# Two causal attentions of a four-layer kernel: the diagonal tiles of the maximum pass go out through ScalarE and GpSimd, and the weighting stands between the two score pairs

## The chip, the core and the metric

One core of a Trainium2 chip runs the whole kernel as one program. Its engines are TensorE (PE in the profile; PEld is its weight load), VectorE (DVE), ScalarE (ACT), GpSimd (POOL) and SyncE (SP, which only starts transfers). The metric is the device time of one execution in microseconds. Attention B_ and attention G_ are the same function, called twice; its tiles carry these letters in the profile.

## The reference

The program computes a grouped-query causal attention, a mixture of experts, an attention in which masks go by pages of 64 positions, and two layers of local attention with a gated unit, with layer norms between. The change touches only the first and the third. What they compute, for 2 sequences of 2048 positions and 16 heads of 16 columns:

```python
att = jnp.einsum('bsgmd,btgd->bgmst', q, k) / scale
att = jnp.where(causal, -jnp.inf, att)            # third layer: pages[None, :] <= pages[:, None] is kept
att = jax.nn.softmax(att, axis=-1)
ctx = jnp.einsum('bgmst,btgd->bsgmd', att, v).reshape(b, s, DIM)
```

## The kernel before, in words

`attention` works in 8 iterations, one for each sequence and group of 4 heads. Each iteration does two things for its four heads. First, scores with queries on partitions (tiles `pm`), of which only the maximum of each query over its keys is wanted; it is later subtracted through two extra rows of the query operand. Second, scores with keys on partitions (`psc`), their exponential (`p`, by ScalarE), and the weighting of the values into `po` (`weigh`). The queries and keys are stored as high and low parts stacked to 48 rows (50 with the maxima), heads alternating between partitions 0 and 64.

The second part is cut into 40 steps: four query chunks of 512, and for chunk qc the 4(qc+1) key blocks of 128 up to the diagonal. In the last four key blocks of a chunk the step is 512, 384, 256 and 128 columns wide. The first part is cut into tiles ("pieces") of one head by up to 512 keys, or two heads where the width is at most 256. A list `ring` holds the 144 pieces of an iteration in order of query block, and between them, for each chunk, a "fold" (VectorE brings the partial maxima together, GpSimd splits them into high and low part) and, 12 pieces after the chunk's last one, a "turn" (TensorE transposes them, ScalarE copies them out, SyncE sends them into the rows of the query operand). The pieces run 22 entries ahead: `cut[t]` gives the entries of step t, 3 or 4 of them, and the first 83 stand in an opening before the first step. Pieces and turns take three PSUM banks in rotation (`RING = 3`, `slots`); `free` makes TensorE wait until the former user of the bank has been read. One bank holds `po`; `psc` takes four.

TensorE's order in step t is: first score pair (heads 0 and 1), one ring entry, second score pair (heads 2 and 3), one ring entry, the weighting of step t-1, the other entries (lines 454 to 465). The score pair waits for the exponential of the same pair in the step before; the weighting waits for both exponentials of step t-1, in diagonal steps also for GpSimd's clearing of `p` (line 304 or 308), and in a chunk's first step for the copy of `po`.

VectorE takes the pieces in the same order. A piece that ends at the diagonal gets a `tensor_tensor_reduce` with a mask tile `far` for each head (line 510, followed in the profile by an accumulator read), any other one a plain maximum (line 515). The copy of `po` to `o` (line 528) stands on VectorE after the entries of a chunk's first step. ScalarE does the exponentials (line 491) and the copies of the turned maxima (line 479). In a step with a turn, SyncE first sends the two transfers of its maxima (line 355) and then, in a chunk's first step, stores the output of the chunk before (line 360); it takes its work strictly in order. In the fifth step GpSimd starts the 13 loads of the next iteration.

Of the kernel before, what the change touches and what calls it, by code (L numbers as in the profile page):

```python
# [6 lines left out]
F32 = mybir.dt.float32  # L7
# [8 lines left out]
P = 128  # L16
# [162 lines left out]
def attention(nc, sem, tag, nk, page, qh, ql, kh, kl, vs, mask_qk, ident_bf, ident, ot):  # L179
# [5 lines left out]
    AHEAD = 22  # L185

# [4 lines left out]
    pieces = []  # L191
    for qb in range(NQ):
        full, rest = divmod((qb + 1) * P, CH)
        for kc in range(full + (rest > CH // 2)):
            pieces += [(qb, kc, min(CH, (qb + 1) * P - kc * CH), [h]) for h in range(GRP)]
        if 0 < rest <= CH // 2:
            pieces += [(qb, full, rest, [u, u + 2]) for u in range(2)]
    NP = len(pieces)
    steps = [(qc, kb) for qc in range(NC4) for kb in range(SUB * (qc + 1))]
    NS = len(steps)  # L200
    closes = [max(j for j, pc in enumerate(pieces) if pc[0] // SUB == c) for c in range(NC4)]
    ring = []
    for j in range(NP):
        ring.append(("piece", j, 0))
        for behind, kind in ((1, "fold"), (12, "turn")):
            for c in range(NC4):
                if (closes[c] + behind) % NP == j:
                    ring.append((kind, c, (closes[c] + behind) // NP))
    NE = len(ring)
    slots, taken = [], 0  # L210
    for kind, _, _ in ring:
        slots.append(taken % RING)
        taken += kind != "fold"
    cut = [NE * (t + AHEAD) // NS for t in range(NS + 1)]

    def exists(k, e):

        return not isinstance(k, int) or 0 <= k - ring[e][2] < NIT

    def spread(i, t):  # L220

        return [(i + e // NE, e % NE) for e in range(cut[t], cut[t + 1]) if exists(i + e // NE, e % NE)]

    opening = [(0, e) for e in range(cut[0]) if exists(0, e)]

    with ExitStack() as ctx:
# [6 lines left out]
        mpart = sb("mpart", [P, 2, PAR, NQ, NC4], F32)  # L233
        mfold = sb("mfold", [P, 2, PAR, SUB], F32)
        m = sb("m", [P, P], F32R)
        mrow = sb("mrow", [2 * GRP * SUB, P], F32)
        one = sb("one", [2, CH], F32)
        mqk = sb("mqk", [P, P], BF16)
        far = sb("far", [P, CH], F32)
# [6 lines left out]
        m_mask, far_set, apart = sem(tag + "m_mask", 0), sem(tag + "far_set"), sem(tag + "apart")  # L246
        q_in = [sem(f"{tag}q_in{i}", 0) for i in range(2)]
        s_max, max_done = sem(tag + "s_max"), sem(tag + "max_done")
        folded, m_hi, m_all = sem(tag + "folded"), sem(tag + "m_hi"), sem(tag + "m_all")
# [29 lines left out]
        def _(pool):  # L279

            pool.dma_start(mqk[:], mask_qk).then_inc(m_mask, 16)
# [37 lines left out]
            def split(k, e, clears):  # L319
                kind, c, late = ring[e]  # L320
                if kind != "fold":
# [3 lines left out]
                wait_apart(pool, folded, (k - late) * NC4 + c + 1, fence)  # L325
                wait_apart(pool, mt_done, (k - late) * NC4 + c, fence)
                parts = m[:, 0:2 * GRP * SUB].rearrange("p (b r n) -> p r b n", b=2, r=2)
                whole = mfold[:].rearrange("p b a j -> p b (a j)")
                pool.tensor_copy(parts[:, 0], whole).then_inc(m_hi, 1)
                wait_apart(pool, m_hi, (k - late) * NC4 + c + 1, fence)  # L330
                pool.tensor_tensor(parts[:, 1], whole, parts[:, 0].bitcast(F32), ALU.subtract).then_inc(m_all, 1)
                wait_apart(pool, m_all, (k - late) * NC4 + c + 1, fence)

            for k, e in opening:
                split(k, e, None)

            def body(i, s, half):
                for t, (qc, kb) in enumerate(steps):
# [5 lines left out]
                    for k, e in spread(i, t):  # L344
                        split(k, e, i * NQ + masked(t + 1))
# [3 lines left out]
        def _(sp):  # L349
            def m_row(k, e, s):  # L350
                _, c, late = ring[e]
                sp.wait_ge(mr_done, (k - late) * NC4 + c + 2)
                s = (s + late) % 2
# [8 lines left out]
            for k, e in opening:  # L362
                if ring[e][0] == "turn":
                    m_row(k, e, 0)

            def body(i, s, half):
                for t, (qc, kb) in enumerate(steps):
                    for e in range(cut[t], cut[t + 1]):
                        if ring[e % NE][0] == "turn" and exists(i + e // NE, e % NE):
                            m_row(i + e // NE, e % NE, (s + e // NE) % 2)  # L370
# [11 lines left out]
        def _(pe):  # L382
            def free(k, e):

                for back in range(1, 2 * NE):
                    g = e - back
                    kk, n = k + g // NE, g % NE
                    if ring[n][0] != "fold" and slots_at(g) == slots[e] and exists(kk, n):
                        break
                    if isinstance(kk, int) and kk < 0:  # L390
                        return
                kind, j, late = ring[n]
                if kind == "piece":
                    pe.wait_ge(max_done, kk * NP + j + 2)
                else:
                    pe.wait_ge(mr_done, (kk - late) * NC4 + j + 2)

            def slots_at(g):

                return slots[g % NE]  # L400

            def event(k, e, s):
                kind, j, late = ring[e]
                if kind == "fold":
                    return
# [30 lines left out]
            def body(i, s, half):  # L436
                for t, (qc, kb) in enumerate(steps):
# [22 lines left out]
                    elif not static(i, 0):  # L460
                        weigh(i - 1, 1 - s, NS - 1)
# [1897 lines left out]
```

## Time and profile before

| | us |
|---|---|
| median of 3 runs | 5498.16 (5486.85 to 5507.22) |
| profiled execution | 5505.85 |
| its span, first to last instruction | 5504.3 |
| TensorE busy in the span | 4333.2 (79%) |
| VectorE busy | 3117.9 (57%) |
| ScalarE busy | 2342.5 (43%) |
| GpSimd busy | 1217.9 (22%) |

Busy time is the union of an engine's instructions; matmuls are pipelined, so TensorE's share overstates how much its array works. The granted clock of TensorE is given as a share of full speed. In a row, `A<-B,C` says which tile is written from which, and a bracket gives the idle time of the engine before the row and what ended it. Several instructions of a kind that follow each other are merged into one row with their number at its end.

### The profile page before, as it was taken

The numbers are of one execution on the slowest core, as the hardware profiler recorded it, in microseconds if no ns is written. First come the engines' busy times: TensorE is split into PE (matmuls) and PEld (weight loads), VectorE is DVE, ScalarE is ACT, GpSimd is POOL, SyncE is SP. The second block draws the span as 40 slices with busy tenths as digits, with TensorE's granted clock in tenths as the row PEclk, the third lists the DMA queues.
The fourth block names the chain that finished last, engine by engine and source line by source line (L and its number), as shares of the span: only waits on it lengthen the run. The fifth ranks groups of instructions, "written<-read, shape, count | busy, mean of one in ns | idle before, by whom it ended". The sixth has DMA issues, their size and how long they took to land. (4 is left out here: it accounts for less than half of the span.)

```text
span 5504.3 us, 82496 instructions
## 1 busy us (share of the span) xinstructions
PE 4333.2 (79%) x24804; PEld 2724.9 (50%) x24804; DVE 3117.9 (57%) x6686; ACT 2342.5 (43%) x4143; POOL 1217.9 (22%) x1610
## 2 busy tenths in 40 slices
PE   4899999952989995649989899657796976689687
PEld 2433433341888884324333334345565755566466
DVE  1787777641444442648777777267454437656444
ACT  1365555621444442214555555323454433355333
POOL 1011111015000002110111110123585003378300
PEclk9788878875999997777878776789898988899888
DMA  7211311023112112352223330233453113345211
GB/s 219 33 29 32 48 31 28 11 101 115 57 49 76 47 48 67 118 129 32 40 40 49 49 57 11 90 108 116 150 157 110 31 48 107 120 156 158 69 34 35
DMA packets 327165, 413.82 MB, mean 75 GB/s; under 512 B 40804, under 2 KB 236257, under 8 KB 323260
## 3 DMA queue, kind: packets, MB, share of 16 engines
q1 hardware_dynamic: 278620, 257.43, 14.9%
q0 software_dynamic: 43616, 148.19, 12.7%
q10 hardware_dynamic: 4608, 4.20, 0.2%
q8 instruction: 167, 2.74, 0.2%
q14 instruction: 154, 1.26, 0.1%
HBM read 252.64 MB, written 156.19 MB: 74 GB/s over the span
## 5 line engine op out<-in xcount | busy, mean ns | idle before, releaser
L491 ACT ACTIVATE G_p<-G_psc 128x1024 f32<-128x1024 f32 (+3 forms) x640 | 541.9, 894 | 426.0 <-PE G_psc L454 423.6
L491 ACT ACTIVATE B_p<-B_psc 128x1024 f32<-128x1024 f32 (+3 forms) x640 | 541.7, 894 | 370.7 <-PE B_psc L454 367.9
L515 DVE TENSOR_REDUCE G_mpart<-G_pm 128x1 f32<-128x512 f32 x768 | 485.2, 684 | 150.0 <-PE G_pm L416 148.2
L416 PE MATMUL G_pm<-G_ks,G_qs 48*128 48x512 f32 (+3 forms) x1280 | 491.2, 521 | 89.3 <-DMA G_ks<-G_one 58.7
L515 DVE TENSOR_REDUCE B_mpart<-B_pm 128x1 f32<-128x512 f32 x768 | 483.8, 684 | 98.6 <-PE B_pm L416 96.5
L416 PE MATMUL B_pm<-B_ks,B_qs 48*128 48x512 f32 (+3 forms) x1280 | 480.1, 506 | 74.5 <-DMA B_ks<-B_one 42.9
L1705 POOL TENSOR_SCALAR J_pr<-J_pr,J_rc 128x256 f32<-128x256 f32 x512 | 462.7, 915 | 41.2 <-DVE J_rc L1843 38.8
L416 PEld LDWEIGHTS G_pm<-G_ks,G_qs 48*128 48x128 f32 x1280 | 229.9, 227 | 478.4 <-DVE G_mpart L515 222.9
L416 PEld LDWEIGHTS B_pm<-B_ks,B_qs 48*128 48x128 f32 x1280 | 222.8, 218 | 450.4 <-DVE B_mpart L515 223.6
L431 PE MATMUL G_po<-G_p,G_v 128*32 128x512 f32 (+3 forms) x2560 | 371.2, 657 | 20.5 <-DVE G_o L528 18.9
L431 PE MATMUL B_po<-B_p,B_v 128*32 128x512 f32 (+3 forms) x2560 | 353.3, 628 | 21.9 <-DVE B_o L528 19.3
L454 PE MATMUL G_psc<-G_qs,G_ks 50*128 50x512 f32 (+3 forms) x1280 | 334.5, 452 | 41.9 <-DMA G_qs<-G_mrow 31.9
L454 PE MATMUL B_psc<-B_qs,B_ks 50*128 50x512 f32 (+3 forms) x1280 | 324.9, 440 | 13.3 <-issue 7.7
L510 DVE CUSTOM_DVE_ANT_0 G_pm<-G_pm,G_far 128x384 f32<-128x384 f32 (+3 forms) x512 | 238.8, 517 | 125.6 <-PE G_pm L416 124.4
L1060 ACT ACTIVATE E_hs<-E_pH,E_bf 128x512 f32<-128x512 f32 (+1 forms) x192 | 115.7, 602 | 434.6 <-PE E_pG L1014 434.6
L510 DVE CUSTOM_DVE_ANT_0 B_pm<-B_pm,B_far 128x384 f32<-128x384 f32 (+3 forms) x512 | 238.9, 518 | 105.7 <-PE B_pm L416 104.2
L1027 PE MATMUL E_pO<-E_wp,E_a 128*128 128x256 f32 (+1 forms) x1920 | 252.0, 296 | 57.8 <-DVE E_a L1089 52.3
L1574 POOL TENSOR_TENSOR I_t<-I_qn,I_R 128x512 f32<-128x512 f32 x128 | 166.7, 1323 | 512.8 <-DVE I_qn L1628 512.8
L1027 PEld LDWEIGHTS E_pO<-E_wp,E_a 128*128 128x128 f32 (+1 forms) x1920 | 246.7, 198 | 63.1 <-DVE E_a L1089 57.2
L1014 PE MATMUL E_pH<-E_xT,E_wfg 128*128 128x512 f32 (+1 forms) x1152 | 262.4, 364 | 19.7 <-DVE E_wfg L1099 15.6
L1014 PE MATMUL E_pG<-E_xT,E_wfg 128*128 128x512 f32 (+1 forms) x1152 | 255.7, 358 | 0.0
L1804 ACT ACTIVATE J_pr<-J_pS,J_nm 128x256 f32<-128x256 f32 x512 | 234.8, 477 | 38.9 <-DVE J_nm L1839 38.8
(307 smaller groups left out, 7962.1 us busy)
## 6 DMA issues: line engine op xcount, KB each, us to landing
J_v<-lve SPq DMA_DIRECT2D x64, 520.0 KB, 3.8
J_k<-lkT SPq DMA_DIRECT2D x64, 512.0 KB
lve<-I_v SPq DMA_DIRECT2D x64, 260.0 KB, 2.1
lqT<-I_tT SPq DMA_DIRECT2D x64, 256.0 KB, 2.4
lkT<-I_tT SPq DMA_DIRECT2D x64, 256.0 KB, 2.6
J_q<-lqT SPq DMA_DIRECT2D x64, 256.0 KB
ein<-Z_z SPq DMA_DIRECT2D x8, 1228.0 KB
E_xin<-ein POOLq DMA_DIRECT2D x8, 1152.0 KB, 6.3
```

Of the source, the lines that this page charges most:

```text
L416: last = pe.matmul(t[:, n * w:(n + 1) * w], qs[s][rows, qb // SUB, h // 2, qb % SUB * P:(qb % SUB + 1) * P], ks[s][rows, h // 2 % NA, kc * ...
L431: last = pe.matmul(po[VW * h:VW * (h + 1), off:CH], v[s][:, kb, h % nk], p[:, t % 2, h, off:CH], start=kb == 0, stop=kb == SUB * (qc + 1) - 1,
L454: score = pe.matmul(psc[:, h, off:CH], ks[s][rows, h // 2 % NA, kb * P:(kb + 1) * P], qs[s][rows, qc, h // 2, off:CH], start=True, stop=True)
L491: act.activation(p[:, t % 2, 2 * pr:2 * pr + 2, off:CH], psc[:, 2 * pr:2 * pr + 2, off:CH], ACT.Exp, scale=SC).then_inc(e_done[pr], 1)
L510: last = dve.tensor_tensor_reduce(pm[slots[e]][:, x * w:(x + 1) * w], pm[slots[e]][:, x * w:(x + 1) * w], far[:, CH - w:CH], 1.0, -3e38, A ...
L515: dve.tensor_reduce(mpart[:, heads[0] % 2, heads[0] // 2, qb, kc:kc + 1], pm[slots[e]][:, 0:w], AX, ALU.max).then_inc(max_done, 1)
L1014: last = pe.matmul(bank[ht % 2][:, 0:w], wfg_p[pw][:, i, kc, ht * P:(ht + 1) * P], xT[px][:, kc, 0:w], start=kc + j == 0, stop=kc == KC - ...
L1027: last = pe.matmul(pO[j // 2][0:r, j % 2 * D:(j % 2 + 1) * D], a[pa][:, ht, j * P:j * P + r], wp_p[pw][:, ht], start=ht + i == 0, stop=ht ...
L1060: act.activation(hs[:, ht % 2, 0:w], pH[ht % 2][:, 0:w], ACT.Identity, bias=bf[:, s, ht:ht + 1]).then_inc(hs_done, 1)
L1574: last = pool.tensor_tensor(t2[:, u, :, :, a:a + H], qn[:, u, :, :, z:z + H], R[:, :, ds(w_, 1), a:a + H].to_broadcast([P, 2, LH, H]), ALU ...
L1705: last = pool.tensor_scalar(pr[:, u, pos(h)], pr[:, u, pos(h)], rc[:, u, pos(h):pos(h) + 1], None, ALU.mult)
L1804: last = act.activation(pr[:, u, pos(h)], pS[:, pos(h)], ACT.Exp, bias=nm[:, u, pos(h):pos(h) + 1], scale=8.0, accum_out=su[:, u, pos(h):p ...
```

## The change

- The ring no longer has masked pieces. The pieces end before the diagonal block; the diagonal blocks of two query blocks and two heads form one entry "diag": four matmuls of 128 columns in one bank. An iteration has 128 pieces, 16 diagonal entries and 4 turns, 148 entries in all; folds are no entries any more.
- A diagonal entry is copied by ScalarE into one of four tiles `dm` in SBUF (`d_out`), masked there by GpSimd (`d_cut`; `affine_select` in B_, fills in G_), and VectorE takes its maximum, 512 columns at once, six entries later (`d_max`). ScalarE's copy frees the bank.
- The partial maxima get a fifth column per query block for the diagonal. Mask tile, mask transfer and `tensor_tensor_reduce` go; `wait_apart` goes from VectorE.
- Within the entries of a step the pieces come first, then diagonal entries and turns.
- TensorE's order in a step is: first score pair, one entry, the weighting of step t-1, second score pair, the other entries.
- ScalarE copies `po` out after the exponentials of a chunk's first step, ahead of its copies of diagonal entries and turns.
- The turn of the third chunk falls into the fifth step instead of the sixth, that of the first into the 25th instead of the 26th, that of the second into the 33rd instead of the 34th.

The core of the diff:

```diff
+    DSLOTS = 4
+    REDUCE_BEHIND, TURN_BEHIND = 6, 12
...
+        for kc in range(qb // SUB):
+            off += [("piece", (qb, kc, CH, [h])) for h in range(GRP)]
+        rest = qb % SUB * P
+        if rest > CH // 2:
+            off += [("piece", (qb, qb // SUB, rest, [h])) for h in range(GRP)]
+        elif rest:
+            off += [("piece", (qb, qb // SUB, rest, [u, u + 2])) for u in range(2)]
+        if qb % 2 == 0:
+            off = [("diag", (qb, 0))] + off[:2] + [("diag", (qb, 1))] + off[2:]
...
+        held = [order[e % NE] for e in range(cut[t], cut[t + 1])]
+        held = [x for x in held if x[0] == "piece"] + [x for x in held if x[0] != "piece"]
...
+            def cut_diagonal(k, e, clears):
+                if ring[e][0] != "diag" or not exists(k, 0):
                     return
+                d = number[e]
+                if clears is not None:
+                    wait_apart(pool, cleared, clears, fence)
+                wait_apart(pool, d_out, k * ND + d + 1, fence)
+                tile = dm[:, d % DSLOTS]
+                if page == 1:
+                    pool.affine_select(out=tile, in_=tile, pattern=[[0, 2 * PAR], [-1, P]], compare_op=ALU.is_ge,
+                                       fill=-3e38, base=0, channel_multiplier=1).then_inc(d_cut, 1)
...
+                if kind == "diag":
+                    qb, u = what
+                    parts = [(h, q, q * P, P) for h in (u, u + 2) for q in (qb, qb + 1)]
...
                         score.then_inc(s_done, 1)
-                        some(pr, pr + 1)
-                    if t:
-                        weigh(i, s, t - 1)
-                    elif not static(i, 0):
-                        weigh(i - 1, 1 - s, NS - 1)
-                    some(2, len(events))
+                        if pr == 0:
+                            some(0, 1)
+                            if t:
+                                weigh(i, s, t - 1)
+                            elif not static(i, 0):
+                                weigh(i - 1, 1 - s, NS - 1)
+                    some(1, NE)
...
+                if kind == "diag":
+                    d = number[e]
+                    act.wait_ge(s_max, k * NI + issued[e] + 2)
+                    if not static(k, 0) or d >= DSLOTS:
+                        act.wait_ge(d_max, k * ND + d + 2 - DSLOTS)
+                    act.activation(dm[:, d % DSLOTS], pm[slots[e]][:].rearrange("p (n k) -> p n k", k=P), ACT.Copy
+                                   ).then_inc(d_out, 1)
...
+            def copy_out(i, qc):
+                act.wait_ge(pv_done, i * NS + sum(SUB * (c + 1) for c in range(qc + 1)) + 1)
...
+                act.activation(o[:, qc % 2], po[:], ACT.Copy).then_inc(o_done, 1)
```

## Rows read from the trace of the kernel before

**Rows 1.** The page: busy time, share of the span, instructions of each engine.

```profile
PE 4333.2 (79%) x24804; PEld 2724.9 (50%) x24804; DVE 3117.9 (57%) x6686; ACT 2342.5 (43%) x4143; POOL 1217.9 (22%) x1610
```

**Rows 2.** Windows: us, busy us (instructions) per engine, granted clock, DMA share, GB/s.

```profile
149.50:197.20 47.70, 46.14 (x96) 24.10 (x97) 46.02 (x135) 0.53 (x2) 0.82 (x4) 0.50 0.40 46
...
197.20:1110.00 912.80, 846.15 (x5060) 354.45 (x5056) 692.01 (x1722) 546.70 (x670) 139.93 (x266) 0.84 0.17 28
...
2522.70:3493.00 970.30, 877.82 (x5060) 366.49 (x5056) 693.04 (x1722) 546.95 (x670) 97.70 (x266) 0.79 0.22 36
...
610.54:651.16 40.62, 38.48 (x259) 15.88 (x258) 36.18 (x90) 28.67 (x35) 3.19 (x7) 1.00 0.02 8
...
2968.70:3009.31 40.61, 38.45 (x259) 15.89 (x258) 36.17 (x90) 28.78 (x34) 1.65 (x6) 1.00 0.03 9
...
572.00:578.30 6.30, 5.58 (x41) 2.50 (x41) 6.30 (x14) 3.93 (x5) 0.63 (x1) 1.00 0.00 0
...
578.40:588.50 10.10, 10.10 (x44) 4.24 (x38) 5.20 (x12) 4.05 (x5) 0.00 (x0) 0.50 0.08 28
...
653.60:680.60 27.00, 26.06 (x115) 10.99 (x114) 17.25 (x40) 11.53 (x16) 10.31 (x19) 0.50 0.65 86
```

**Rows 3.** Timeline of B_, a high-clock step: start, us, engine, work [idle before].

```profile
705.31 0.50 PE L416 MATMUL B_pm<-B_ks,B_qs 48*128 48x512 f32 x2
...
705.64 0.40 PE L454 MATMUL B_psc<-B_qs,B_ks 50*128 50x512 f32 x2
...
705.84 1.29 DVE L515 TENSOR_REDUCE B_mpart<-B_pm 128x1 f32<-128x512 f32 x2 [0.21 <-PE B_pm L416]
...
706.08 1.94 ACT L491 ACTIVATE B_p<-B_psc 128x1024 f32<-128x1024 f32 x2 [0.75 <-PE B_psc L454]
...
706.59 0.50 PE L416 MATMUL B_pm<-B_ks,B_qs 48*128 48x512 f32 x1
...
707.02 1.06 PE L431 MATMUL B_po<-B_p,B_v 128*32 128x512 f32 x8
...
708.01 0.50 PE L416 MATMUL B_pm<-B_ks,B_qs 48*128 48x512 f32 x2
```

**Rows 4.** Timeline of B_, a low-clock step.

```profile
674.89 0.79 PE L416 MATMUL B_pm<-B_ks,B_qs 48*128 48x512 f32 x2
...
675.49 0.63 PE L454 MATMUL B_psc<-B_qs,B_ks 50*128 50x512 f32 x2
...
675.72 2.48 DVE L515 TENSOR_REDUCE B_mpart<-B_pm 128x1 f32<-128x512 f32 x4 [1.83 <-PE B_pm L416]
...
676.47 0.79 PE L416 MATMUL B_pm<-B_ks,B_qs 48*128 48x512 f32 x1
...
677.19 1.93 PE L431 MATMUL B_po<-B_p,B_v 128*32 128x512 f32 x8
...
679.06 0.79 PE L416 MATMUL B_pm<-B_ks,B_qs 48*128 48x512 f32 x2
```

**Rows 5.** Timeline of B_ where a query chunk begins.

```profile
576.95 0.69 DVE L528 COPY B_o<-B_po 128x512 f32<-128x512 f32 x1
...
577.78 1.42 PE L431 MATMUL B_po<-B_p,B_v 128*32 128x512 f32 x8 [0.72 <-DVE B_o L528]
```

**Rows 6.** Timeline of G_, SyncE's queue, then TensorE.

```profile
2903.62 1.31 SPq L355 DMA_DIRECT2D G_qs<-G_mrow  x2
...
2929.46 1.21 PE L454 MATMUL G_psc<-G_qs,G_ks 50*128 50x512 f32 x3 [5.72 <-DMA G_qs<-G_mrow]
```

**Rows 7.** Groups by line and form: busy us, mean ns | idle before, releaser.

```profile
L510 DVE CUSTOM_DVE_ANT_0 B_pm<-B_pm,B_far 128x512 f32<-128x512 f32 x128 | 86.0, 715 | 23.4 <-PE B_pm L416 22.8
...
L510 DVE DVE_READ_ACCUMULATOR2_ANT B_mpart<- 128x1 f32 x512 | 72.7, 142 | 0.0
...
L1810 ACT ACTIVATE J_pT<-J_pP 128x512 f32<-128x512 f32 x128 | 76.4, 597 | 276.3 <-PE J_pP L1763 276.3
...
L304 POOL TENSOR_SCALAR_AFFINE_SELECT B_p<-B_p 128x512 f32<-128x512 f32 x128 | 81.2, 634 | 467.8 <-ACT B_p L491 464.9 <-POOL B_m L331 2.9
```

More of the change, by code:

```diff
@@ L220, in spread @@
-    def spread(i, t):
-        return [(i + e // NE, e % NE) for e in range(cut[t], cut[t + 1]) if exists(i + e // NE, e % NE)]
-    opening = [(0, e) for e in range(cut[0]) if exists(0, e)]
+    order, close = [], {}
+    for qb in range(NQ):
+        off = []
+        for kc in range(qb // SUB):
[7 more added lines that the diff above has]
+            off = [("diag", (qb, 0))] + off[:2] + [("diag", (qb, 1))] + off[2:]
+        order += off
+        close[qb // SUB] = len(order) - 1
@@ new lines, in attention @@
+    NE = len(order) + NC4
+    late_of = {}
+    for c in reversed(range(NC4)):
+        at = close[c] + TURN_BEHIND
+        late_of[c] = int(at >= len(order))
+        order.insert(at % len(order), ("turn", c))
+    cut = [NE * (t + AHEAD) // NS for t in range(NS + 1)]
+    ring = [None] * NE
+    for t in range(NS):
+        held = [order[e % NE] for e in range(cut[t], cut[t + 1])]
+        held = [x for x in held if x[0] == "piece"] + [x for x in held if x[0] != "piece"]
+        for x, e in zip(held, range(cut[t], cut[t + 1])):
+            ring[e % NE] = x
@@ new lines, in attention @@
+    late = [late_of[x[1]] if x[0] == "turn" else 0 for x in ring]
+    number, count = [], {"piece": 0, "diag": 0, "turn": 0}
+    for kind, what in ring:
+        number.append(what if kind == "turn" else count[kind])
+        count[kind] += 1
+    NP, ND = count["piece"], count["diag"]
+    issued = [sum(x[0] != "turn" for x in ring[:e]) for e in range(NE)]
+    NI = NP + ND
+    slots = [e % RING for e in range(NE)]
+    if NE % RING == 1:
+        slots[-1] = 1
+    after = [[] for _ in range(NE)]
@@ new lines, in attention @@
+    last_of = {c: (0, 0, 0) for c in range(NC4)}
+    for e, (kind, what) in enumerate(ring):
+        if kind == "diag":
+            after[(e + REDUCE_BEHIND) % NE].append(("reduce", e, (e + REDUCE_BEHIND) // NE))
+        if kind != "turn":
+            c = what[0] // SUB
+            ready_at, pieces_done, diags_done = last_of[c]
+            if kind == "piece":
+                last_of[c] = (max(ready_at, e), number[e] + 1, diags_done)
+            else:
+                last_of[c] = (max(ready_at, e + REDUCE_BEHIND), pieces_done, number[e] + 1)
@@ L226, in attention, with exists, window @@
+    for c in range(NC4):
+        e = last_of[c][0] + 1
+        after[e % NE].append(("fold", c, e // NE))
+    def exists(k, back):
+        return not isinstance(k, int) or 0 <= k - back < NIT
+    def window(i, t):
+        return [(i + e // NE, e % NE) for e in range(cut[t], cut[t + 1])]
+    opening = [(0, e) for e in range(cut[0])]
     with ExitStack() as ctx:
@@ L362, in _ @@
             for k, e in opening:
-                if ring[e][0] == "turn":
+                if ring[e][0] == "turn" and exists(k, late[e]):
                     m_row(k, e, 0)
@@ L367, in body @@
                 for t, (qc, kb) in enumerate(steps):
-                    for e in range(cut[t], cut[t + 1]):
-                        if ring[e % NE][0] == "turn" and exists(i + e // NE, e % NE):
-                            m_row(i + e // NE, e % NE, (s + e // NE) % 2)
+                    for x in range(cut[t], cut[t + 1]):
+                        k, e = i + x // NE, x % NE
+                        if ring[e][0] == "turn" and exists(k, late[e]):
+                            m_row(k, e, (s + x // NE) % 2)
                     if kb == 0:
@@ L524, in copy_out @@
-            def copy_out(i, qc):
-                dve.wait_ge(pv_done, i * NS + sum(SUB * (c + 1) for c in range(qc + 1)) + 1)
-                if not (isinstance(i, int) and i == 0 and qc < 2):
-                    dve.wait_ge(o_out[qc % 2], i * (NC4 // 2 * 16) + qc // 2 * 16 + 1)
-                dve.tensor_copy(o[:, qc % 2], po[:]).then_inc(o_done, 1)
-            dve.memset(mpart[:], -3e38)
-            dve.memset(far[:], 0.0).then_inc(far_set, 1)
-            dve.wait_ge(far_set, 2)
-            dve.wait_ge(m_mask, 16)
```

204 lines of the change are left out of this document (93 added, 111 removed).

## The prediction

> **What bounds the kernel now.** I read the page first (VectorE busy 3117.9 of 5504.3 us, TensorE 4333.2) [rows 1]: neither share names a bound. Both attentions together last, after their openings, 912.8 + 970.3 us, and only they and their openings (47.7 us in B_) are touched by the change [rows 2]. Each holds 8 iterations of 40 steps, so an iteration takes 912.8/8 = 114.1 us in B_ (granted clock 0.84) and 121.3 us in G_ (0.79) [rows 2]. The clock has two levels, 2.4 and 1.2 GHz, so B_ spends 2 x (1 - 0.84) = 0.32 of its time at the low one, G_ 0.42. The last 16 steps of an iteration run wholly at the high level, in 40.6 us [rows 2], 2.54 us a step.
>
> What ends last in a step is in the timeline of one ordinary step [rows 3]. In each step TensorE issues a first score pair (S0), a maximum tile (ev0), the second pair (S1), ev1, the weighting W of the step before, ev2, ev3. Maximum tiles go through a ring of three banks, so ev1 of the next step takes the bank of this step's ev2. The reader should follow one circle: ev2 starts at 705.31; VectorE starts its maximum at 705.84 (0.53 later), and ev1 starts at 706.59, when that maximum is done and the bank released (0.75 later, 1.28 in all); W follows 0.43 later, at 707.02; the next ev2 0.99 later, at 708.01. Sum 2.70 us, exactly the step. TensorE and VectorE both look nearly full, but the pace is that of this circle of bank, maximum and weighting. At the low clock the same circle is 1.58 + 0.72 + 1.87 = 4.17 us (674.89 to 676.47 to 677.19 to 679.06) [rows 4]. Steps with three tiles instead of four have no such circle through W and are shorter.
>
> **The change part by part.** *VectorE.* Masked maxima (0.67 us for 512 columns, 86.0/128) become plain ones (0.64, half of the 1.29 for two) over about the same columns [rows 3, 7]. What goes is their accumulator read, 64 an iteration at 72.7/512 = 0.14 us, 9 us, some 3 of it beside the next maximum, and the four copies of the output, 0.69 each [rows 5, 7]: some 9 us of the 692.0/8 = 86.5 us that VectorE works in an iteration [rows 2]. As it isn't what closes the circle, I count this at nothing in ordinary steps; in steps with 512-column diagonal tiles it is already within the mean below.
>
> *ScalarE.* 16 evictions and 4 output copies an iteration at 0.60 (76.4/128) [rows 7] make 12 us on top of 546.7/8 = 68.3 [rows 2]: 80 of over 107, not the bound. An eviction stands behind the second exponential and delays the next first one; S1 needs that only in the step after, about 2.9 us away, so it is covered. *GpSimd.* A mask is 0.63 us (81.2/128) [rows 7], or fills for G_; the maximum follows six tiles, about 1.6 steps or 4.5 us, behind the matmuls, and eviction plus mask end about 2.9 us after S1 starts (0.54 + 1.02 + 0.60 + 0.63 + 0.1). Covered by 1.5 us; the loads that keep GpSimd 8 us in the fifth step meet no diagonal tile, since the written order has none from the fourth to the ninth window. If the cover fails, VectorE waits and the following tile's bank comes late, up to 1 us for each of 16 tiles.
>
> *TensorE, tiles.* 208 matmuls replace 160 for the maxima, with the same columns. A diagonal tile is four 128-column matmuls: between one slot of 512 columns (0.24) and four (0.96) [rows 3]. I take 0.5, nearest to one slot plus exposed weight loads. It stands last in its window; between ev1 and the next ev0 TensorE has 1.18 us in which it must wait anyway, so 0.24 + 0.5 + 0.24 is hidden. At 0.96 it sticks out by 0.26 us in 16 windows: 4 us an iteration, 64 in all, for the range.
>
> *The weighting between the pairs.* The order becomes S0, ev0, W, S1, ev1, ev2, ev3. The ring still holds three banks, so in a window of four tiles the next ev0 takes ev1's bank, and this is the new circle: S1 starts 0.99 after W; ev1 0.33 after that (the distance from the first pair after W, 705.31, to the next, 705.64); the maximum starts 0.43 later (0.53 less the 0.10 of weight load that only the first pair after W shows); maximum and release 0.75 (705.84 to 706.59); then W 0.43 later. Sum 0.99 + 0.33 + 0.43 + 0.75 + 0.43 = 2.93 us, against 2.70: the second score pair now stands inside the circle [rows 3]. At the low clock: 1.87 + 0.60 + 0.67 + 0.75 + 0.72 = 4.6 against 4.17 (the 0.60 is 674.89 to 675.49, the 0.67 is 0.83 less the first weight load, here 0.16) [rows 4]. In windows of three another circle appears: W needs the second exponential of the step before, which needs S1, which now follows the former W: 0.53 + 1.02 (half of the 1.94 for two, with the overlap) + 0.07 + 0.99 = 2.62 us [rows 3]. At the low clock TensorE's own sum is longer: 0.43 + 0.72 + 1.87 + 0.60 + 0.43 = 4.05 (0.43 for a pair, 512 columns at 1.2 GHz) [rows 4].
>
> The written order has 148 tiles in 40 windows: 28 windows of four and 12 of three. High clock: 28 x 2.93 + 12 x 2.62 = 113.5; the diagonal steps are 384, 256 and 128 columns wide, which shortens W (4 columns' time each) and S1 by 1.6 us in each of four query chunks, 6.4; narrow tiles take off 1; in the first step of each chunk ScalarE's copy of the output stands behind the second exponential and W waits for it, 0.6 more, about 1.7 in four. Together 107 us. Low clock: 28 x 4.6 + 12 x 4.05 = 177, less 12.8 and 2, is 162.
>
> *Waits that go.* The output copy stood in VectorE's queue behind diagonal maxima: W waited for it, 0.72 us idle [rows 5]. And in G_ the row of maxima for the third chunk is sent at 2903.62, behind an output store, while the next iteration's loads run; the first scores of that chunk wait 5.72 us for it, until 2929.46 [rows 6]. The change puts this turn one window earlier and so ahead of that store in SyncE's queue. I let this stall go: my 107 and 162 hold none. If it stays, 5.7 x 6 = 34 us come back. Next late there is then nothing but the circle.
>
> *The clock.* It fell at 578.4, right after the wait for the output copy [rows 2, 5], and is low at the start of an iteration, as from 653.6 to 680.6 (the last steps before that are narrow ones); it came back after ordinary low-clock steps, in which TensorE waited little [rows 2, 4]. The change removes some of the waits before a fall, but stretches every ordinary step at equal matmul work (2.70 to 2.93, 4.17 to 4.6), so TensorE pauses more in each. I take the low share from 0.32 to 0.38 in B_ and from 0.42 to 0.45 in G_. An iteration is then 1/(0.62/107 + 0.38/162) = 122.9 us in B_ and 1/(0.55/107 + 0.45/162) = 126.5 in G_: (122.9 - 114.1) x 8 + (126.5 - 121.3) x 8 = 70 + 42 = +112 us. Of this 48 + 28 = 76 would come with unchanged shares. The openings, where VectorE is busy 46.0 of 47.7 us [rows 2], save some 3 us each: -6.
>
> Sum: the profiled execution has 5505.85 us (span 5504.3); +106 makes 5612. It lies 7.7 above the median of the runs, 5498.16; against that the forecast is 5605.
>
> The rule in the Trainium skill that speaks against the change stands in "TensorE: Matmul & The Clock Gate", section "A second HAM failure mode: psum-queue depth-cycling": short pauses of TensorE between matmul groups, while it cycles through PSUM banks, make its clock swing between the levels. By it the low share would rise, the first rival below. In this trace ordinary steps with a bank wait held the high clock (last 16 steps at 1.00), so the rule alone did not decide here before.
>
> **The rivals.** *The clock falls far more* (the cited rule's case): the longer pauses keep it low after each iteration's start. At a low share of 0.6 in both, 134.6 us an iteration: 8 x (20.5 + 13.3) - 6 = +264, 5762. For it: the openings, with VectorE setting the pace and pauses in every tile, stay at 0.50 throughout [rows 2]. Against it: fewer long waits.
>
> *Fewer falls outweigh the circle* (the other side): each fall follows a long wait, and the output-copy and row stalls were these. At a low share of 0.2 in both, 1/(0.8/107 + 0.2/162) = 114.8 us: 8 x (0.7 - 6.5) - 6 = -52, 5446. It turns faster once the share is under about 0.25 in both. For it: 572.0 to 578.3 at 1.00, then 0.50 for 10 us [rows 2]; against it: the narrow steps, after which the longest low stretches come (0.50 for 27 us from 653.6 [rows 2]), stay.
>
> *VectorE's relief counts*: if the circle is looser than I think (say a pair slips past the bank wait), half of the 9 us reaches each iteration: -72, 5426. The Trainium skill's "TensorEngine Tiling (Array Packing)", section "PSUM Bottleneck", advises sharing PSUM eviction between both engines, and is for this case. Against it: the circle explained 2.70 to the hundredth.
>
> **How the numbers follow.** Forecast case (5540 to 5680) 0.48; clock far lower 0.25; fewer falls 0.19; VectorE's relief 0.08. What can be told from no change is 0.5%, 27 us. Slower: all of the first two, 0.73, less a little; faster: most of the last two, 0.18; within 0.5%: 0.10 from the edges. The range of 8 in 10 is 5460 to 5760: below it takes in much of the faster cases, above it the 64 and 34 us and nearly the clock rival. The forecast's own range is 5540 to 5680.
>
> **What would show it.** In an ordinary full-clock window of four tiles, W to W at 2.93 us, with TensorE waiting for VectorE's maximum ahead of ev0; three-tile windows near 2.62 with W behind the exponential; the last 16 steps at 43.8 instead of 40.6; VectorE busy about 9 us less an iteration; no 5.7 us wait for the row in G_. Wrong would be ordinary steps of 2.6 or less, or a low-clock share far from 0.38 and 0.45.

## The result, and the profile after

Slower, by far more than forecast. The changed kernel takes 5893.01 us (median of 4 runs, 5842.27 to 5900.21) against 5492.51 for the kernel before (4 runs): ratio 1.0713, 95% interval 1.0655 to 1.0772. The forecast was 5605, with 8 chances in 10 between 5460 and 5760. The profiled execution is the fastest of the changed kernel, 5842.27 us, and lies 336.4 above that of before (5505.85); the other runs have a mean granted clock of 0.788 to 0.790 over the whole execution, this one 0.804, and take about 50 us more.

Windows of the changed kernel, columns as in [rows 2]: the opening of B_, the eight iterations of B_ and of G_.

```profile
149.00:198.70 49.70, 46.26 (x131) 29.11 (x131) 45.21 (x80) 7.59 (x14) 8.39 (x16) 0.50 0.38 43
198.70:1334.10 1135.40, 1034.48 (x5407) 451.50 (x5403) 651.10 (x1105) 630.26 (x817) 213.60 (x382) 0.69 0.14 23
2752.70:3835.30 1082.60, 973.58 (x5407) 428.24 (x5403) 650.42 (x1105) 629.59 (x817) 133.36 (x382) 0.75 0.20 32
```

Against [rows 2], B_ took 222.6 us more, G_ 112.3, the opening 2.0: together 336.9, so nothing of the 336.4 is left for the rest of the program. The granted clock fell from 0.84 to 0.69 in B_ and from 0.79 to 0.75 in G_, so the share of time at the low level, 2 x (1 - clock), rose from 0.32 to 0.62 and from 0.42 to 0.50. (Shares below are worked out like this.) VectorE's busy time fell from 692.0 to 651.1.

Timeline of B_ after: an ordinary step from W (B_po) to W, 653.82 to 656.75, and the first step with a diagonal block behind it. Columns as in [rows 3].

```profile
653.82 1.06 PE L485 MATMUL B_po<-B_p,B_v 128*32 128x512 f32 x8
...
654.82 0.50 PE L507 MATMUL B_psc<-B_qs,B_ks 50*128 50x512 f32 x2
...
655.15 0.40 PE L470 MATMUL B_pm<-B_ks,B_qs 48*128 48x512 f32 x2
...
655.59 2.48 DVE L580 TENSOR_REDUCE B_mpart<-B_pm 128x1 f32<-128x512 f32 x4 [0.46 <-PE B_pm L470]
...
656.33 0.49 PE L470 MATMUL B_pm<-B_ks,B_qs 48*128 48x512 f32 x1 [0.31 <-DVE B_mpart L580]
...
656.75 1.06 PE L485 MATMUL B_po<-B_p,B_v 128*32 128x512 f32 x8
...
658.30 1.72 ACT L560 ACTIVATE B_p<-B_psc 128x1024 f32<-128x1024 f32 x2 [1.00 <-PE B_psc L507]
...
659.49 0.63 POOL L337 TENSOR_SCALAR_AFFINE_SELECT B_p<-B_p 128x512 f32<-128x512 f32 x1 [10.56 <-ACT B_p L560]
660.17 0.16 PEld L485 LDWEIGHTS B_po<-B_p,B_v 128*32 128x32 f32 x8 [1.48 <-POOL B_p L337]
660.18 1.06 PE L485 MATMUL B_po<-B_p,B_v 128*32 128x512 f32 x8 [1.33 <-POOL B_p L337]
```

The first of the two is the predicted circle, to the hundredth: second score pair 1.00 after W, tile 0.33 later, maximum 0.44 later, bank back 0.74 later, W 0.42 later: 2.93. The second is a circle that the forecast didn't have. W waits 1.33 us for GpSimd's clearing of `p` (L337), which can start only when ScalarE's second exponential is done, and that stands behind S1, which now follows W: 3.43 us in all. Before, S1 stood ahead of W and the clearing had that time.

Waits of the changed kernel over the whole execution (engine line <- releaser: us in total, times, longest us):

```profile
PEld B_po L485 <- POOL B_p L337: 83.5, 112, 2.2
PEld G_po L485 <- POOL G_p L341: 46.1, 78, 1.9
PE B_po L485 <- POOL B_p L337: 42.9, 71, 1.6
...
PE G_psc L507 <- DMA G_qs<-G_mrow: 15.9, 5, 4.7
```

and the same view of the kernel before:

```profile
PE B_po L431 <- DVE B_o L528: 19.3, 29, 1.0
...
PEld B_po L431 <- POOL B_p L304: 6.0, 14, 0.8
...
PE G_psc L454 <- DMA G_qs<-G_mrow: 31.9, 5, 10.0
```

In B_ the wait of W's weight loads (PEld) for GpSimd went from 14 small ones to 112; the PE row of 42.9 us is the same waiting, seen at the matmuls. The wait for the output copy of [rows 5] is gone, the stall on the row of maxima of [rows 6] is halved.

Windows of the changed kernel over the last 16 steps of an iteration: the second, fourth and eighth of B_, then the eighth of G_.

```profile
427.49:475.31 47.82, 43.56 (x278) 20.22 (x278) 35.49 (x61) 32.37 (x41) 7.18 (x13) 0.93 0.02 7
709.29:765.70 56.41, 52.68 (x278) 24.20 (x277) 35.25 (x60) 32.81 (x41) 7.18 (x13) 0.71 0.02 6
1272.02:1334.17 62.15, 45.77 (x198) 11.58 (x198) 0.00 (x0) 29.05 (x33) 3.19 (x5) 0.50 0.01 4
...
3775.27:3836.05 60.78, 45.77 (x198) 11.59 (x198) 0.00 (x0) 29.32 (x34) 1.53 (x5) 0.50 0.01 5
```

Before, these steps ran wholly at the high level in 8 of the 16 iterations, in 40.6 us where maxima are left [rows 2]; the prediction took them to do so in all. Now that happens in none. The last two rows are the plainest case, because no maximum tiles are left there: 198 matmuls with no bank wait and no VectorE. The same 198 of the kernel before:

```profile
1074.98:1108.85 33.87, 30.38 (x198) 8.58 (x196) 0.86 (x2) 27.91 (x32) 2.54 (x4) 0.90 0.03 9
3461.46:3492.50 31.04, 27.96 (x198) 8.19 (x196) 1.21 (x2) 27.83 (x32) 1.23 (x4) 1.00 0.03 10
```

These two stretches alone cost (62.15 - 33.87) + (60.78 - 31.04) = 58 us of the 336. The timeline of the changed kernel in the first of them says how:

```profile
1291.29 1.94 PE L485 MATMUL B_po<-B_p,B_v 128*32 128x512 f32 x8 [0.79 <-ACT B_p L560]
...
1293.15 1.22 PE L507 MATMUL B_psc<-B_qs,B_ks 50*128 50x512 f32 x4
1293.99 1.94 ACT L560 ACTIVATE B_p<-B_psc 128x1024 f32<-128x1024 f32 x2 [1.94 <-PE B_psc L507]
...
1295.16 1.94 PE L485 MATMUL B_po<-B_p,B_v 128*32 128x512 f32 x8 [0.79 <-ACT B_p L560]
```

In each step of 3.87 us TensorE waits 0.79 us for the exponentials and works the rest, at the low level. Before, a step of the same 12 matmuls took some 2.0 us (31.04 to 33.87 over 16). The 1.9 us more are of two kinds, a longer loop of scores, exponential and weighting, and the low level; experiment 4 shows the same loop at the high level and so tells them apart.

### The profile page after: what moved, and what is told of

It reads as the page before. It is cut to its first block and busy times, and to the rows that moved or that the text cites. A ratio compares the mean times of both kernels' runs of the same rounds, so it can differ in the third digit from the quotient of the medians.

```text
span 5840.7 us, 83726 instructions
## 1 busy us (share of the span) xinstructions
PE 4613.9 (79%) x25572; PEld 2888.3 (49%) x25572; DVE 3033.0 (52%) x5338; ACT 2525.1 (43%) x4463; POOL 1339.4 (23%) x1864
## 5 line engine op out<-in xcount | busy, mean ns | idle before, releaser
L580 DVE TENSOR_REDUCE B_mpart<-B_pm 128x1 f32<-128x512 f32 (+3 forms) x1024 | 622.7, 652 | 429.8 <-PE B_pm L470 427.7
L580 DVE TENSOR_REDUCE G_mpart<-G_pm 128x1 f32<-128x512 f32 (+3 forms) x1024 | 622.1, 652 | 396.9 <-PE G_pm L470 395.6
L470 PE MATMUL G_pm<-G_ks,G_qs 48*128 48x512 f32 (+3 forms) x1664 | 452.6, 431 | 96.1 <-DMA G_ks<-G_one 58.0
L485 PE MATMUL B_po<-B_p,B_v 128*32 128x512 f32 (+3 forms) x2560 | 421.7, 742 | 64.6 <-POOL B_p L337 42.9
L507 PE MATMUL B_psc<-B_qs,B_ks 50*128 50x512 f32 (+3 forms) x1280 | 440.2, 564 | 9.0 <-issue 9.0
L507 PE MATMUL G_psc<-G_qs,G_ks 50*128 50x512 f32 (+3 forms) x1280 | 415.7, 535 | 23.2 <-DMA G_qs<-G_mrow 15.9
L470 PEld LDWEIGHTS B_pm<-B_ks,B_qs 48*128 48x128 f32 x1664 | 308.8, 254 | 190.6 <-DVE B_mpart L580 121.3
L470 PEld LDWEIGHTS G_pm<-G_ks,G_qs 48*128 48x128 f32 x1664 | 292.9, 241 | 213.7 <-DVE G_mpart L580 129.7
L507 PEld LDWEIGHTS B_psc<-B_qs,B_ks 50*128 50x128 f32 x1280 | 207.0, 248 | 364.0 <-issue 354.7
L507 PEld LDWEIGHTS G_psc<-G_qs,G_ks 50*128 50x128 f32 x1280 | 195.4, 233 | 351.9 <-issue 343.0
```

Source lines behind the costliest of these rows:

```text
L470: last = pe.matmul(t[:, n * w:(n + 1) * w], qs[s][rows, q // SUB, h // 2, q % SUB * P:(q % SUB + 1) * P], ks[s][rows, h // 2 % NA, first:f ...
L485: last = pe.matmul(po[VW * h:VW * (h + 1), off:CH], v[s][:, kb, h % nk], p[:, t % 2, h, off:CH], start=kb == 0, stop=kb == SUB * (qc + 1) - 1,
L507: score = pe.matmul(psc[:, h, off:CH], ks[s][rows, h // 2 % NA, kb * P:(kb + 1) * P], qs[s][rows, qc, h // 2, off:CH], start=True, stop=True)
L580: dve.tensor_reduce(mpart[:, heads[0] % 2, a:z, qb, kc], pm[slots[e]][:, 0:len(heads) * w].rearrange("p (h k) -> p h k", k=w), AX, ALU.max ...
```

## The experiments

Two causes stood against each other: the pace of the step (order, clearing, narrow matmuls) and the clock's share. All ratios are to the kernel before, measured in the same series; its medians there were 5504.12, 5477.05 and 5482.4 us.

**1. The old order in the changed kernel**

```
-                        if pr == 0:
-                            some(0, 1)
-                            weigh(...)
-                    some(1, NE)
+                        some(pr, pr + 1)
+                    weigh(...)
+                    some(2, NE)
```

> The changed kernel with TensorE's old order in a step (first pair, entry, second pair, entry, weighting, the rest); the diagonal tiles still go through ScalarE and GpSimd. Theory 1 (the order is the cost: it puts the second score pair, and in diagonal steps GpSimd's clearing, into the circle, and the pauses lower the clock): ordinary four-tile steps return from 2.93 to 2.70 us at the high clock, the clock in the attentions to about 0.82, the time to 5400 to 5520 us. Theory 2 (the diagonal tiles' new path through ScalarE, GpSimd and four narrow matmuls is the cost): still above 5750 us.

5367.56 us (5355.32 to 5381.70), ratio 0.9753 (0.9704 to 0.9803), below the expected 5400 to 5520. Its windows, B_, G_, and the 198 matmuls without maxima in each:

```profile
198.60:1079.60 881.00, 849.78 (x5406) 386.24 (x5403) 645.76 (x1105) 614.01 (x818) 212.93 (x382) 0.85 0.18 29
2489.30:3369.50 880.20, 823.24 (x5406) 373.72 (x5403) 645.47 (x1105) 614.73 (x818) 133.24 (x382) 0.88 0.25 40
...
1047.85:1079.60 31.75, 27.90 (x198) 8.17 (x196) 0.00 (x0) 28.47 (x34) 2.55 (x4) 1.00 0.03 9
3338.00:3369.50 31.50, 28.04 (x198) 8.23 (x196) 0.00 (x0) 28.81 (x34) 1.23 (x4) 1.00 0.03 10
```

All of the loss goes, and a gain of 2.5% is left. The low share is 0.30 and 0.24, the 198 matmuls run at the high level throughout, and an ordinary step is 2.70 us again, as its timeline has it (W at 326.29 and 328.99):

```profile
326.29 1.07 PE L485 MATMUL B_po<-B_p,B_v 128*32 128x512 f32 x8
...
328.99 1.06 PE L485 MATMUL B_po<-B_p,B_v 128*32 128x512 f32 x8
```

**2. The new order alone, in the kernel before** (the reverse of edit 1, there)

> The kernel before with only the new order in a step (weighting between the score pairs). Theory 1 (order): above 5800 us, four-tile steps at 2.93 at the high clock, granted clock in the attentions near 0.70. Theory 2 (diagonal path): within 1% of the kernel before, 5440 to 5550 us.

5928.07 us, ratio 1.0776 (1.0705 to 1.0846), as expected by theory 1. Its windows, B_, G_, and the same 198 matmuls in each:

```profile
195.50:1362.70 1167.20, 997.27 (x5059) 395.47 (x5056) 692.90 (x1721) 560.22 (x670) 140.26 (x266) 0.70 0.14 22
2783.30:3925.90 1142.60, 979.05 (x5059) 388.87 (x5056) 692.01 (x1722) 560.12 (x670) 97.80 (x266) 0.72 0.19 31
...
1301.10:1362.70 61.60, 45.72 (x198) 11.54 (x198) 0.69 (x1) 28.56 (x32) 3.18 (x5) 0.50 0.01 5
3865.61:3925.90 60.29, 45.76 (x198) 11.55 (x198) 0.98 (x2) 28.56 (x32) 1.53 (x5) 0.50 0.01 5
```

Experiments 1 and 2 show it from both sides: the order costs 8% with the old tiles (1.0776) and 10% with the new ones (5893.01/5367.56), and under the old order the rest of the change earns 2.5%. The low shares are 0.60 and 0.56.

**3. The clearing taken out of the changed kernel.** The causal cut of the weighting's input is left out, and with it W's wait for it.

```
-                    if kb >= SUB * qc:
-                        clear(i, t)
...
-                if kb >= SUB * qc:
-                    pe.wait_ge(cleared, i * NQ + masked(t) + 2)
```

> The changed kernel without GpSimd's clearing of the exponentials in diagonal steps and without the weighting's wait for it; this leaves the causal cut out of the weighting. Theory 1a (the clearing, now inside the circle, is a large part of the loss that the prediction missed): the diagonal steps of B_ shorten by about 0.7 us and those of G_ by 0.4, and the time falls by 120 to 200 us, to 5690 to 5770. Theory 1b (the loss is the clock, which falls from the pauses of ordinary steps, and the clearing is small): down by less than 60 us, 5830 or more.

5813.78 us, ratio 1.0578 (1.0523 to 1.0634): 80 us less than the changed kernel, between the figures of the two sides. Its windows:

```profile
201.20:1272.20 1071.00, 993.98 (x5407) 440.63 (x5403) 649.66 (x1105) 631.74 (x818) 131.87 (x254) 0.73 0.15 24
2689.80:3801.60 1111.80, 1014.90 (x5406) 447.92 (x5403) 650.52 (x1105) 631.43 (x818) 93.76 (x254) 0.71 0.20 31
```

The pace can be compared place by place: I take a step from the first matmul of one W to that of the next, keep the steps that ran at a granted clock of 1.00 throughout, and take their mean for each of the 40 places of an iteration. 28 places of B_ and 31 of G_ have such steps in both kernels; without the clearing they are 4.5 us shorter in B_ and 1.9 in G_, added up. The step that ends in a chunk's first W with a clearing fell from 3.42 to 2.71 us in B_ and from 3.08 to 2.71 in G_, the 0.7 and 0.4 of theory 1a. The time fell by less than that theory's 120 us, and by more than theory 1b's 60. The profiled executions, both at a mean granted clock of 0.804, are only 32 us apart (5842.27 and 5810.71), and of the attentions B_ got shorter (1135.4 to 1071.0) and G_ longer (1082.6 to 1111.8), with low shares of 0.54 and 0.58 against 0.62 and 0.50. So some 30 us of the 80 are seen as pace; the rest probably goes with the clock, which differs from one execution to the next.

**4. The first score pair issued twice, in the changed kernel.** The same scores are written once more: two matmuls more in each of the 320 steps of an attention, and nothing is shortened.

```
-                        for h in (2 * pr, 2 * pr + 1):
+                        for h in (2 * pr, 2 * pr + 1) * (2 - pr):
```

> The changed kernel with the first score pair of each step issued twice (same operands, same result): 1280 more matmuls, in the place where TensorE waits for the bank of the next maximum. If the clock falls because TensorE has too little to do in the longer steps, the granted clock of the attentions rises from 0.70 in B_ to 0.8 or more and the time falls to 5600 to 5780 us although work was added. If the clock has another cause, the time stays within 1% of the changed kernel's 5893 or grows by up to 100 us (at most 0.24 us in each of 640 steps).

5721.03 us, ratio 1.0417 (1.0347 to 1.0486): 3% less than the changed kernel, for more work. Its windows:

```profile
199.20:1251.60 1052.40, 959.58 (x6044) 466.05 (x6041) 648.77 (x1105) 632.59 (x817) 212.74 (x382) 0.82 0.15 25
2665.80:3712.40 1046.60, 957.70 (x6044) 465.39 (x6041) 649.98 (x1105) 631.41 (x818) 133.01 (x382) 0.82 0.21 34
```

The high-clock ordinary step is still 2.93 to 2.94, and over the 27 places of B_ and 32 of G_ that ran at the high level in both kernels the steps add up to the same time within 0.1 us: no pace was gained. The low share is 0.36 in both, near that of the kernel before (0.32 and 0.42). The run splits the loss: about 172 us of the changed kernel's time is clock that the added matmuls give back, net of what they cost in low-clock steps, and some 220 us over before stay at shares like before's, which is pace.

The last 16 steps of B_ and of G_, without maxima, and three rows of the timeline in B_:

```profile
1202.96:1250.94 47.98, 34.22 (x220) 11.91 (x220) 0.00 (x0) 28.77 (x33) 2.54 (x4) 0.82 0.02 6
3663.79:3711.35 47.56, 35.54 (x220) 12.28 (x221) 0.00 (x0) 28.67 (x33) 1.23 (x4) 0.79 0.02 6
...
1209.91 1.94 PE L485 MATMUL B_po<-B_p,B_v 128*32 128x512 f32 x8 [0.36 <-ACT B_p L560]
...
1216.48 1.06 PE L485 MATMUL B_po<-B_p,B_v 128*32 128x512 f32 x8 [0.74 <-ACT B_p L560]
...
1219.19 1.06 PE L485 MATMUL B_po<-B_p,B_v 128*32 128x512 f32 x8 [0.75 <-ACT B_p L560]
```

At the low level the step is 3.87 us as without the doubling, but TensorE now waits 0.36 us in it and not 0.79. In B_ the clock rose after two such steps, and the next nine, of 2.70 us, ran at 1.00 although each has a wait of 0.75. So of the 3.87 us in the changed kernel, against 2.0 before, the longer loop is 0.7 and the low level 1.2. It also shows that a wait of this length in each step doesn't by itself bring the clock down.

**5. The same doubling in the kernel before, and in the kernel of experiment 1**

> The kernel before with the first score pair of each step issued twice. Control for the doubling in the changed kernel: if that gained 3% by filling TensorE's pauses, then here, where an ordinary step has a pause of 0.25 us at the high clock and 0.13 us at the low one, it gains little and costs up to 0.3 us in low-clock steps: 5450 to 5600 us, the low-clock share somewhat smaller than 0.32 and 0.41. If doubling helps for another reason (whatever the pauses), it gains 3% here as well, below 5400.

5426.49 us, ratio 0.9914 (0.9887 to 0.9941), low shares 0.20 and 0.26 (clock 0.90 and 0.87). Below the expected range: it gains 0.9%, where I had expected the added columns to cost at least as much as they gave.

> The changed kernel with TensorE's old order and the first score pair issued twice. By the pauses: within 1.5% of the same kernel without the doubling (5368 us), since its low-clock share is already 0.30 and 0.24 and its pauses are short. If more work always lifts the clock: below 5300 us.

5321.79 us, ratio 0.9713 (0.9674 to 0.9752), the fastest median of all. Its windows:

```profile
199.70:1060.10 860.40, 837.37 (x6044) 420.31 (x6041) 645.76 (x1105) 615.75 (x818) 212.08 (x382) 0.92 0.19 30
2450.10:3326.20 876.10, 831.75 (x6043) 418.04 (x6041) 646.15 (x1105) 616.03 (x818) 133.04 (x382) 0.92 0.25 40
```

Within the expected 1.5%. A low share of 0.16 in both is bought with pace: the mean high-clock steps, added over the 40 places, are 99.3 us in G_ against 97.4 in experiment 1 (in B_ five places never ran high there). Hence only 0.4% better than that one by the ratios, within the two intervals.

**6. The clearing taken out of the kernel before** (edit 3, there)

> The kernel before without GpSimd's clearing of the exponentials and the weighting's wait for it; this leaves the causal cut out of the weighting. Control for the same edit in the changed kernel, which gained 80 us: if the clearing costs only where the weighting stands between the score pairs, the time here stays within 0.5% of the kernel before. If the clearing costs in any order (an engine's load, not its place in the circle), it gains 60 us or more here too.

5461.83 us over 10 runs, ratio 0.9977 (0.9950 to 1.0004). As expected if its place counts and not its load: in the old order the clearing costs nothing that can be told from noise (at most 0.5%); it is the new order that puts it on the path.

**7. The output copies alone moved to ScalarE, in the kernel before**

```
-                dve.tensor_copy(o[:, qc % 2], po[:]).then_inc(o_done, 1)
+                act.activation(o[:, qc % 2], po[:], ACT.Copy).then_inc(o_done, 1)
```

> The kernel before with one part of the change alone: the output copies go from VectorE to ScalarE, ahead of its copies of the maxima. If the 2.5% that the new diagonal path wins under the old order comes mostly from the weighting no longer waiting behind masked maxima in VectorE's queue (19 us of waits in each attention, and a clock fall after some): 5430 to 5465 us. If it comes from the masked maxima themselves and from the turn's earlier place: within 0.4% of the kernel before, 5480 to 5520.

5407.04 us, ratio 0.9867 (0.9824 to 0.9909), better than expected. It is half of what experiment 1 earns; what earns the other half (masked maxima gone, order of the tiles, earlier turns) was not taken apart. Of the four steps of an iteration that end in a chunk's first W, which waited for the copy [rows 5], three ran at the high level in both kernels in B_: they took 3.25 to 3.36 us and now take 2.29 to 2.39.

**8. The second maximum tile ahead of the second score pair, in the changed kernel** (order S0, ev0, W, ev1, S1, ev2, ev3)

```
                                 weigh(i - 1, 1 - s, NS - 1)
-                    some(1, NE)
+                            some(1, 2)
+                    some(2, NE)
```

> The changed kernel with a second maximum tile between the weighting and the second score pair (first pair, tile, weighting, tile, second pair, the rest). The second pair is then outside the circle of bank and maximum, which returns to 2.70 us; but the second exponential starts 0.33 later and the weighting waits for it: 0.99 + 0.33 + 0.43 + 1.02 + 0.07 = 2.84 us for every ordinary step at the high clock, three-tile steps too. Time 5700 to 5880. If the circle is not what sets the pace, four-tile steps stay at 2.93 or fall to 2.7.

5865.20 us, ratio 1.0722 (1.0680 to 1.0764). The time lies in the expected range, the step does not: I expected 2.84 for the ordinary one, it stayed at 2.93 to 2.94. With ev1 ahead the bank circle is shorter, but S1 comes later, and the loop of S1, second exponential and W takes its place: in B_ the matmuls of W wait for an exponential 120 times (49.6 us in all), against 37 times (19.3 us) in the changed kernel. That loop is 0.1 longer than I reckoned, as in steps of three tiles (2.71, not 2.62).

**9. Old order with another rotation of the banks.** The skip that the rotation of three banks needs once an iteration is put at the third chunk's turn; then with the first pair doubled, then with both.

```
-    slots = [e % RING for e in range(NE)]
-    if NE % RING == 1:
-        slots[-1] = 1
+    turn2 = ring.index(("turn", 2))
+    slots = [e % RING if e < turn2 else (e - 1) % RING for e in range(NE)]
+    slots[turn2] = slots[turn2 - 2]
```

> The changed kernel with TensorE's old order, and the place where the rotation of three banks skips (148 entries are not a multiple of 3) moved from the last entry, a 384-column piece with a diagonal entry behind it, to the turn of the third chunk. If the skip is what makes the 18th and 19th step long (2.74 and 3.53 us at the high clock), they come to about 2.70 and 2.70 and the time falls by 10 to 25 us from 5368. If not, nothing moves.

5368.17 us, ratio 0.9819 (0.9758 to 0.9880): the two steps, counted from the start of one first exponential to the next, got shorter (medians 2.74 to 2.59 and 3.53 to 3.22; 2.70 was expected for both), but the time is that of experiment 1.

> The former one with the first score pair issued twice as well. The two gains add up if they are of different kinds: 5290 to 5315 us. If the clock's share is already what it can be, no gain over the kernel with the skip moved alone, and 5340 or more.

5330.55 us (5286.60 to 5342.15), ratio 0.9752 (0.9700 to 0.9803): between the two expectations, 0.7% below the kernel with the skip moved alone, of the same series (5368.17 us, with ranges that don't overlap), and no better than the doubling without the new rotation (5321.79). The low shares of the profiled execution were 0.06 and 0.16.

> As before, but both score pairs issued twice, 2560 extra matmuls. The second doubled pair stands before the wait for ev1's bank too, but the pause there (0.25 us) is already filled: at the high clock each step gets up to 0.23 us longer where TensorE is full. If the pace decides: slower than with one doubled pair, 5340 to 5450 us. If the clock's share decides: below 5290.

5361.24 us, ratio 0.9780 (0.9725 to 0.9835). The low shares are no lower than with one pair doubled, 0.09 and 0.15, and the mean high-clock steps, added over the 40 places, are 103.2 us instead of 100.0 in B_ and 102.8 instead of 99.6 in G_: the second doubling is longer than the pause it fills. The time is within the 5340 to 5450 expected if the pace decides.

## Why the prediction was wrong

**What held.** The sign, and the circle: 2.93 at the high level and 4.59 at the low one, predicted 2.93 and 4.6. The masks by GpSimd stayed covered: no wait for one is among the listed waits of VectorE. The range's upper end, though, was the clock rival's 5762, and that rival was the one that came: shares of 0.62 and 0.50.

**The step that failed first: "I take the low share from 0.32 to 0.38 in B_ and from 0.42 to 0.45 in G_."** Measured, 0.62 and 0.50. With my own 107 and 162 us an iteration and the measured shares, B_ would take 8 / (0.38/107 + 0.62/162) = 1084 us and G_ 8 / (0.50/107 + 0.50/162) = 1031, against the 983 and 1012 that are eight times my 122.9 and 126.5. So the share was mis-sized by 101 + 19 = 120 us in the profiled execution, and most of the other 50 us of the median probably belongs here too, since those runs have a lower clock. My argument counted the causes of falls (a long wait each, some of them removed). What decided was how long the clock stays low: in B_ the clock fell 21 times before and 19 times after, but a low stretch lasted 37 us on average (0.62 x 1135.4 / 19) instead of 14 (0.32 x 912.8 / 21), and the last 16 steps now lost the high level in every iteration. In G_ it fell 19 times before and 22 after, with stretches of 25 us instead of 21. Experiment 4 shows it from the other side: with more matmuls in a step that is as long as without them, the share falls back to 0.36. The rule that I had cited from the Trainium skill ("TensorE: Matmul & The Clock Gate", section "A second HAM failure mode: psum-queue depth-cycling") named this outcome, and I held it down because the last 16 steps of before had a bank wait at 1.00. That was a misreading: they held 1.00 in 8 of the 16 iterations only. The trace agrees with the rule (0.32 to 0.62), with one extension: the stretch without maximum tiles, where the pause is for ScalarE and no PSUM bank is waited for, did the same (0.50 throughout 62.15 us).

**The term that was mis-sized: "Together 107 us."** Beyond the share, the iterations took 1135.4 - 1084 = 51 us more in B_ and 1082.6 - 1031 = 52 in G_: 103 us that my pace of an iteration lacked. The low-clock 162 was right: steps wholly at 0.50, one mean for each of the 40 places of B_, add up to 161.6. The high-clock 107 was too small. In the changed kernel only 28 places of B_ have steps wholly at 1.00; they add up to 81.1 us, and the same places took 70.0 before: 11.1 more, where my 107, against the 101.4 that all 40 places of before add up to, allows 5.6. Two causes are seen, the first never priced:

- GpSimd's clearing of `p` came into the circle of S1, second exponential and W: 16 steps an iteration. Experiment 3 puts it at 4.5 us of high-clock pace in B_ and 1.9 in G_ and at 80 us of time in all, experiment 6 at nothing in the old order. I had added up each engine's load (GpSimd turned out busy 26.7 of 141.9 us an iteration in B_), not followed what the moved pair was the start of.
- The loop of exponential and weighting takes 0.1 more than the sum of its rows gave: 2.71 for three tiles, not 2.62, and 2.93 in experiment 8.

The rest is spread over many places and was not taken apart. The narrow matmuls of a diagonal tile are no part of it: at the high level the 27th, 31st and 36th windows of an iteration in B_, of four tiles with a diagonal one, take 2.94 us from W to W, as the 28th and the 34th, with none. They stayed hidden, as forecast, and the 64 us kept for them were not needed.

The prediction's own sums were off a little too. Its terms for the high clock, 113.5 - 6.4 - 1 + 1.7, make 107.8 and not 107, those of the low one 162.6, the three-tile circle 2.61, and 0.55 and 0.45 of 107 and 162 give 126.3 for G_ and not 126.5. Put right, they would have added some 10 us to the forecast.

**The step on the waits: "I let this stall go."** It was halved, from 31.9 to 15.9 us over five waits, so about 16 us came back, within the bound of 34 that I had put on it. The output-copy wait did go, and experiment 7 shows what that copy's move is worth by itself: 1.3%. The openings, counted at -6, gained nothing (49.7 us against 47.7 in B_); VectorE was relieved by 5.1 us an iteration ((692.0 - 651.1) / 8) and not 9.

**VectorE's relief** was a rival at 0.08, and it was there all along, under the order: experiment 1 is 2.5% faster than before with a low share of 0.30 and 0.24. The Trainium skill's "TensorEngine Tiling (Array Packing)", section "PSUM Bottleneck", advises sharing the eviction between both engines. The trace agrees where the order is left alone (0.9867 in experiment 7, 0.9753 in experiment 1).

The account of the profiled execution: forecast +106, share +120, pace +103, openings and the rest +7 come to the +336 measured. What is not settled is what in a step holds the clock down. Ordinary steps of 2.93 us ran at 1.00 as well (653.82 to 656.75), only less often than those of 2.70, and experiment 4 has steps at 1.00 with the wait of 0.75 us that the low-clock steps of the changed kernel also have. The runs don't separate the length of a pause, the number of pauses and the matmul work between them.

## What to carry to other kernels

When work is moved in TensorE's queue, list everything that the moved instruction starts (here S1, the second exponential, the clearing, the weighting) and close each of these loops, not only the one that bounds now. Price the clock by the pauses and the matmul work in each ordinary step, and not only by the rare long waits: a longer step at equal matmul work is paid twice, in pace and at the low level. And an order and a relief of another engine that come in one change are best timed apart; here one costs 8 to 10% and the other earns 2.5%.

## What the runs showed of the hardware

- Matmuls that compute nothing new, put where TensorE waits anyway, came out faster with each of three kernels: 5893 to 5721, 5477 to 5426, 5368 to 5322 us (the last within the intervals of the two; 5368 to 5331 with the other rotation, both in one series). The granted clock rose from 0.69 to 0.82, 0.84 to 0.90 and 0.85 to 0.92 in B_. Doubling the second pair as well cost more than it gave (5331 to 5361).
- The same 198 matmuls took 31.0 to 31.8 us at a granted clock of 1.00 and 60.3 to 62.2 us at 0.50, depending on the order of the work and the waits that come with it. With a wait of 0.79 us in each step of 3.87 the clock stayed at 0.50 to the end of the attention, in both attentions and with old and new tiles; with two matmuls more and a wait of 0.36 in a step of the same length it rose, and then stayed at 1.00 through nine steps of 2.70 us with waits of 0.75.
